# Experts: the down product transposed, in three f32r passes, its input split by ScalarE and GpSimd

## What is computed

```python
y = einsum('nei,ne,ehi->nh', silu(hg) * hu, cw, Wd)      # 16 experts of 64 hidden features
shared = silu(xf @ Ws_g.T) * (xf @ Ws_u.T) @ Ws_d.T      # one of 128
return x + (x + y + shared)                              # and then the layer norm
```

## Time and profile before

| | |
|---|---|
| median of 3 runs | 646.74 us (644.06 to 647.41) |
| the profiled execution | 647.47 us, its span 645.7 us |
| mean granted TensorE clock | 0.961 |
| TensorE busy | 578.3 us (90%), weight loads 481.1 us |
| VectorE, ScalarE, GpSimd busy | 474.1 us (73%), 277.2 us (43%), 208.1 us (32%) |
| experts stage | first pass at 442.06 us, last residual addition at 637.3 us |

### The profile page before, as it was taken

The page is one execution under the profiler, slowest core; times in us unless marked ns, Lnnn a source line. Parts: engine busy times, 40 slices in busy tenths (PEclk is TensorE's granted clock), DMA queues, the critical chain, the costliest instruction groups (busy, mean ns, idle before and its releaser), DMA issues. The chain is left out here.

```text
span 645.7 us, 17900 instructions
## 1 busy us (share of the span) xinstructions
PE 578.3 (90%) x6280; PEld 481.1 (74%) x6280; DVE 474.1 (73%) x1174; ACT 277.2 (43%) x544; POOL 208.1 (32%) x260
## 2 busy tenths in 40 slices
PE   5769999999999745999999998887999999999994
PEld 5647777787787543777788786676888888888884
DVE  2858977977988645677887887564887887888863
ACT  2365645655654401654655563453233233233220
POOL 4233304414421577324345436732021020120122
PEclk9979999999999975899999999898999999999998
DMA  7222122111211554245446537000010100000000
GB/s 221 63 78 78 37 63 65 59 45 58 65 50 34 153 144 100 70 139 171 123 151 169 140 97 218 11 5 32 2 33 2 33 32 0 32 32 0 18 17 16
DMA packets 43086, 46.13 MB, mean 71 GB/s; under 512 B 5056, under 2 KB 31328, under 8 KB 43024
## 3 DMA queue, kind: packets, MB, share of 16 engines
q1 hardware_dynamic: 41104, 42.57, 22.5%
q0 software_dynamic: 704, 1.92, 1.1%
q10 hardware_dynamic: 1216, 0.79, 0.5%
HBM read 32.48 MB, written 10.94 MB: 67 GB/s over the span
## 5 line engine op out<-in xcount | busy, mean ns | idle before, releaser
L1953 PE MATMUL bank<-xT_hl_c,w_up 128*128 128x512 f32 x432 | 119.6, 413 | 2.4 <-ACTq L67 2.4
L141 POOL TENSOR_TENSOR rstd<-mv,norm_c 128x4 f32<-128x4 f32 x24 | 5.2, 216 | 290.9 <-DVE mv L135 183.7
L1278 DVE TENSOR_REDUCE nmax<-bank 128x4 f32<-128x512 f32 x112 | 72.0, 684 | 27.9 <-PE bank L1434 24.6
L1186 ACT ACTIVATE prob<-bank 128x512 f32<-128x512 f32 x128 | 69.4, 594 | 51.3 <-PE bank L1434 35.6
L1953 PEld LDWEIGHTS bank<-xT_hl_c,w_up 128*128 128x128 f32 x432 | 77.3, 192 | 16.3 <-ACTq L67 2.7
L1875 ACT ACTIVATE sg<-bank 128x512 f32<-128x512 f32 x72 | 43.0, 597 | 106.6 <-PE bank L1953 104.7
L1969 PEld LDWEIGHTS bank<-w_down,hid 128*128 128x128 f32 x576 | 74.4, 191 | 6.0 <-issue 0.5
L1969 PE MATMUL bank<-w_down,hid 128*128 128x128 f32 x576 | 75.6, 275 | 0.0
L1424 PE MATMUL bank<-neg_i,mask 64*128 64x256 bf16 x512 | 52.1, 283 | 15.2 <-ACT prob L1186 6.0
L1908 DVE TENSOR_TENSOR gu<-sg,bank 128x512 f32<-128x512 f32 x64 | 43.8, 685 | 21.7 <-PE bank L1953 10.5
L1912 DVE TENSOR_TENSOR hid<-gu,bank 128x512 f32<-128x512 f32 x64 | 44.0, 687 | 6.5
(11 more groups left out here) (219 smaller groups left out, 1174.1 us busy)
## 6 DMA issues: line engine op xcount, KB each, us to landing
rows<-sum_rows_scratch SPq DMA_DIRECT2D x32, 256.0 KB, 3.2
k_stack<-k_scratch SPq DMA_DIRECT2D x32, 128.0 KB, 2.9
q_stack<-q_scratch SPq DMA_DIRECT2D x32, 128.0 KB, 2.8
k_scratch<-k_part SPq DMA_DIRECT2D x16, 192.0 KB, 2.4
q_scratch<-q_part SPq DMA_DIRECT2D x16, 192.0 KB, 2.5
x<-xT_in SPq DMA_DIRECT2D x8, 256.0 KB, 8.4
mask<-mask_in SPq DMA_DIRECT2D x8, 256.0 KB, 3.0
xres<-x_in SPq DMA_DIRECT2D x8, 256.0 KB, 3.7
```

Source lines behind the costliest of these rows:

```text
L1186: act.activation(prob[:, b % 2, ORDER[n], :, :], (TT0, TT1)[n % 2][:, :], ACT.Exp, scale=XD ** -0.5)\
L1278: dve.tensor_reduce(nmax[:, b, 4 * u:4 * u + 4], (SS0, SS1)[n % 2][:, :].rearrange("p (i k) -> p i k", i=4), AX_X, ALU.max, negate=True).t ...
L1953: mm = pe.matmul(bank[:, :], w_up[:, which, a, c, :], xT_hl[par][:, v, :], start=(n == 0), stop=(n == 2))
```

## The change

The down product is turned round: `w_down` is the weights and the hidden activations move, in three f32r passes of 512 columns a chunk, into `PO` with the features in the partitions. For this `hid` is split: ScalarE copies it into a high f32r part (`hidden_hi`), GpSimd subtracts it to get the low part (`hidden_lo`), both into `hid_hl`, a ring of three chunks. `hid` is now a ring of three as well. Down runs three chunks behind up. Since `PO` is now transposed, ScalarE copies it to `outT` and TensorE turns it back in four transposes into `PF` (`output`), a bank that the preparation of the next groups uses too; the residual addition reads `PF`. `w_down` is split once at the start. The preparation moves: the x2 transposes for group `g + 2` now come in the last chunks of group `g`, and four chunks of the next group come before the residual.

```diff
@@ -1800,6 +1800,7 @@
+    LAG, RING = 3, 3
     with ExitStack() as ctx:
@@ -1812,10 +1813,13 @@
         xT_hl.append(sb("xT_hl_c1", [P, 2, GT], F32R))
+        w_down_hl = sb("w_down_hl", [P, 2, NC, P], F32R)
         xs = sb("xs_c", [P, 2, GS, P])
...
         gu = sb("gu", [P, 2, GT])
-        hid = sb("hid", [P, NC, GT])
+        hid = sb("hid", [P, RING, GT])
+        hid_hl = sb("hid_hl", [P, RING, 2, GT], F32R)
+        outT = sb("outT", [P, GT])
         res, stats, mv, rstd = t["res"], t["stats"], t["mv"], t["rstd"]
@@ -1823,7 +1827,10 @@
         p_g, p_d, a_s = sem("gate_mm", NC), sem("down_mm", NC), sem("silu_ready", NC)
+        p_t, a_o = sem("out_transposed"), sem("outT_copied")
         v_gu, v_hid = sem("gu_ready", NC), sem("hid_ready", CHUNKS)
+        a_h, g_l = sem("hid_hi", NC), sem("hid_lo", NC)
+        w_parts = raw("w_down_parts")
         v_res, g_out, x2_out = sem("res_c_ready", 1 + 2 * GS), sem("out_ready", 4), t["x2_out"]
@@ -1856,17 +1863,33 @@
             g_out.prime(pool)
+            g_l.prime(pool)
...
+            def hidden_lo(g, c):
+                pool.wait_ge(a_h.sem, a_h.at(g, c))
+                pool.tensor_tensor(hid_hl[:, c % RING, 1, :], hid[:, c % RING, :], hid_hl[:, c % RING, 0, :].bitcast(F32),
+                                   ALU.subtract).then_inc(g_l.sem, 1)
...
             def group(g, par, left):
+                for c in range(LAG + 1, NC):
+                    hidden_lo(g, c)
+                if left:
+                    for c in range(LAG + 1):
+                        hidden_lo(g + 1, c)
                 normalise_pool(pool, g, v_res, g_out, res, mv, rstd, norm_c, normed[:, par, :, :],
...
+            pool.wait_ge(w_parts, 1)
+            pool.tensor_tensor(w_down_hl[:, 1], w_down[:, :, :], w_down_hl[:, 0].bitcast(F32), ALU.subtract).then_inc(w_parts, 1)
             normalise_pool(pool, NG - 1, t["x2_res"], x2_out, res, mv, rstd, norm_c, x2[:, NSEQ - GS:, :])
+            for c in range(LAG + 1):
+                hidden_lo(0, c)
             pairs(pool, group)
...
         def _(act):
-            a_s.prime(act)
+            for s in (a_s, a_h, a_o):
+                s.prime(act)
@@ -1874,21 +1897,49 @@
+            def hidden_hi(g, c):
+                done = (v_hid, c - 1) if c else (v_gu, 0)
+                act.wait_ge(done[0].sem, done[0].at(g, done[1]))
+                act.wait_ge(p_d.sem, p_d.at(g, c - RING))
+                act.activation(hid_hl[:, c % RING, 0, :], hid[:, c % RING, :], ACT.Copy).then_inc(a_h.sem, 1)
...
+            def output_copy(g):
+                act.wait_ge(p_d.sem, p_d.at(g, NC - 1))
+                act.wait_ge(p_t.sem, p_t.at(g - 1))
+                act.activation(outT[:, :], PO[:, :], ACT.Copy).then_inc(a_o.sem, 1)
...
             def group(g, par, left):
                 nxt = (g + 1, 1 - par)
-                for c in range(2, NC):
+                for c in range(LAG + 1, NC):
                     silu(g, par, c)
-                    if left and c == 2:
-                        x2T_hi(act, e, *nxt)
-                    if left and c == 3:
+                    hidden_hi(g, c - 1)
+                    if left and c == LAG + 1:
                         logit_tanh(act, e, g + 1)
...
                     copy_weights(act, e, *nxt)
+                hidden_hi(g, NC - 1)
+                if left:
                     silu(*nxt, 1)
...
+                    hidden_hi(g + 1, 0)
+                    silu(*nxt, 2)
+                output_copy(g)
+                if left == 2:
+                    x2T_hi(act, e, g + 2, par)
+                if left:
+                    hidden_hi(g + 1, 1)
+                    silu(*nxt, 3)
+                    hidden_hi(g + 1, 2)
...
+            act.activation(w_down_hl[:, 0], w_down[:, :, :], ACT.Copy).then_inc(w_parts, 1)
             silu(0, 0, 0)
             silu(0, 0, 1)
+            hidden_hi(0, 0)
+            silu(0, 0, 2)
+            x2T_hi(act, e, 1, 1)
+            hidden_hi(0, 1)
+            silu(0, 0, 3)
+            hidden_hi(0, 2)
             pairs(act, group)
@@ -1901,7 +1952,7 @@
                 dve.wait_ge(p_u.sem, p_u.at(g, c))
-                dve.wait_ge(p_d.sem, p_d.at(g - 1, c))
+                dve.wait_ge(g_l.sem, g_l.at(g, c - RING))
                 if c:
@@ -1909,35 +1960,40 @@
                     dve.wait_ge(p_w.sem, p_w.at(g, c - 1))
-                    dve.tensor_tensor(hid[:, c, :], gu[:, k, :], WW[(c - 1) % 2][:, :], ALU.mult).then_inc(v_hid.sem, 1)
+                    dve.tensor_tensor(hid[:, c % RING, :], gu[:, k, :], WW[(c - 1) % 2][:, :], ALU.mult).then_inc(v_hid.sem, 1)
...
                 nxt = (g + 1, 1 - par)
-                for c in range(2, NC):
+                for c in range(LAG + 1, NC):
                     hidden(g, par, c)
-                    if left and c == 2:
-                        x2T_lo(dve, e, *nxt)
-                    if left and c == 3:
+                    if left and c == LAG + 1:
                         expert_scores(dve, e, g + 1)
                         rank_groups(dve, e, g + 1)
-                    if left and c == 5:
+                    if left and c == LAG + 3:
                         select_experts(dve, e, g + 1)
-                    if left and c == 7:
+                    if left and c == LAG + 4:
                         share_weights(dve, e, g + 1)
...
                     hidden(*nxt, 1)
-                dve.wait_ge(p_d.sem, p_d.at(g, NC - 1))
-                residual_dve(dve, g, PO, x2[:, bass.ds(g * GS, GS), :], g_out, v_res, dve_passed, res, stats, mv, times=2.0)
+                    hidden(*nxt, 2)
+                    if left == 2:
+                        x2T_lo(dve, e, g + 2, par)
+                    hidden(*nxt, 3)
+                dve.wait_ge(p_t.sem, p_t.at(g))
+                residual_dve(dve, g, PF, x2[:, bass.ds(g * GS, GS), :], g_out, v_res, dve_passed, res, stats, mv, times=2.0)
...
             hidden(0, 0, 1)
+            hidden(0, 0, 2)
+            x2T_lo(dve, e, 1, 1)
+            hidden(0, 0, 3)
             dve.wait_ge(x2_out.sem, x2_out.at(NG - 1, 3))
...
         def _(pe):
-            for s in (p_g, p_d):
+            for s in (p_g, p_d, p_t):
                 s.prime(pe)
@@ -1959,36 +2015,56 @@
             def down(g, c):
+                pe.wait_ge(g_l.sem, g_l.at(g, c))
                 if c == 0:
-                    pe.wait_ge(v_gu.sem, v_gu.at(g, 0))
-                    pe.wait_ge(v_res.sem, v_res.at(g - 1, 0))
-                else:
-                    pe.wait_ge(v_hid.sem, v_hid.at(g, c - 1))
+                    pe.wait_ge(a_o.sem, a_o.at(g - 1))
+                for n, (a, v) in enumerate(((0, 0), (1, 0), (0, 1))):
+                    mm = pe.matmul(PO[:, :], w_down_hl[:, a, c, :], hid_hl[:, c % RING, v, :],
+                                   start=(c == 0 and n == 0), stop=(c == NC - 1 and n == 2))
+                mm.then_inc(p_d.sem, 1)
...
+            def output(g, freed):
+                pe.wait_ge(a_o.sem, a_o.at(g))
+                pe.wait_ge(*freed)
                 for b in range(GS):
...
-                    mm = pe.matmul(PO[:, b * P:(b + 1) * P], hid[:, c, b * P:(b + 1) * P], w_down[:, c, :],
-                                   start=(c == 0 and b == 0), stop=(c == NC - 1), skip_group_check=True)
-                mm.then_inc(p_d.sem, 1)
+                    mm = pe.transpose(PF[:, b * P:(b + 1) * P], outT[:, b * P:(b + 1) * P], ident32[:, :])
+                mm.then_inc(p_t.sem, 1)
...
                 nxt = (g + 1, 1 - par)
-                for c in range(2, NC):
+                for c in range(LAG + 1, NC):
                     up(g, par, c)
-                    down(g, c - 2)
-                    if left and c == 2:
-                        x2T(*nxt)
-                    if left and c == 3:
+                    down(g, c - LAG)
+                    if left and c == LAG + 1:
+                        pe.wait_ge(v_res.sem, v_res.at(g - 1, 0))
                         expert_logits(pe, e, g + 1)
...
                     transpose_weights(pe, e, g + 1)
+                down(g, NC - 3)
+                if left:
+                    up(*nxt, 1)
                 down(g, NC - 2)
                 if left:
-                    up(*nxt, 1)
+                    up(*nxt, 2)
+                if left == 2:
+                    x2T(g + 2, par)
                 down(g, NC - 1)
+                if left:
+                    up(*nxt, 3)
+                if not left:
+                    pe.wait_ge(v_res.sem, v_res.at(g - 1, 0))
+                output(g, (e.a_f.sem, e.a_f.at(g + 2)) if left == 2 else (a_c.sem, a_c.at(g + 1)) if left else (a_c.sem, a_c.at(g)))
+                if left:
+                    down(g + 1, 0)
...
             up(0, 0, 1)
+            up(0, 0, 2)
+            x2T(1, 1)
+            up(0, 0, 3)
+            pe.wait_ge(w_parts, 2)
+            down(0, 0)
             pairs(pe, group)
```

## The result

| | before | after |
|---|---|---|
| median of 4 runs each | 647.08 us (644.06 to 647.92) | 689.34 us (687.41 to 694.72) |
| ratio | | 1.0664, 95% interval 1.0623 to 1.0706 |
| profiled execution, its span | 647.47, 645.7 us | 688.5, 686.8 us |
| granted TensorE clock | 0.961 | 0.938 |
| first residual of the experts after the last one of the attention stage | 472.08 - 439.2 = 32.9 us | 484.34 - 441.7 = 42.6 us |

A forecast was written before the change was run, and what follows sets the result against it. TensorE was taken to bound the experts stage, with VectorE close behind. First group +7.3, groups 1 to 5 +27, group 6 +3.5, last -3.4 sum to +34.4 on 647.47: 682 us, range 653 to 698.

The forecast's parts named there:

- The bound: Experts stage: TensorE bounds it at 24.33 us a group; the change takes it to 21.5, below VectorE's 22.7.
- The slack of VectorE: Experts stage: VectorE's stretches sum to 22.7 of 24.33 us, so it allows a gain of 1.6 a group at most.
- T to s, 16.6: From VectorE's start of chunk 4 (T) to the end of the shares (s): 13.3 us plus 3.3 of collisions.
- s to T', 13.1: From the shares' end through transposes, down 8, ScalarE's copies and chunk 3 to the residual: 13.1 us.
- Collisions, 3.3: VectorE's small two-tensor operations in ranks, selection and shares wait for whole GpSimd operations: +3.3 us a group.
- the upper bound of 4.4: Collisions cost up to 4.4 us a group if MAX8 and MATCH_REPLACE wait for GpSimd as well.
- Rival 1: Few collisions: GpSimd mostly misses VectorE's small operations, leaving the chain of waits alone; 660 us, chance 0.21.
- Rival 3: TensorE's clock falls after pauses of about 3 us; +2.0 in each of seven groups, +14, 696 us; chance 0.13.
- The forecast case: Whole kernel: the chain of waits plus collisions makes the period 29.7 us, +5.4, and the time 682 us; chance 0.50.
- The sum: Whole kernel: 7.3 + 27 + 3.5 - 3.4 = +34.4 us on the profiled 647.47, giving 682 us.
- the first group's +7.3: First group: +5.4, less 0.9 without normalisation before it, plus 2.8 for the residual two chunks later in VectorE's order.
- Rivals 2 and 4: 2: VectorE runs without pause at 22.7 us, 634, chance 0.10. 4: period 24.3, time near 647, chance 0.06.

The follow-up runs named there:

- e7: The changed kernel with every down pass run twice, three passes more a chunk: 705.69 us, ratio 1.0918 to the kernel before.
- e5: The kernel before plus eight GpSimd subtractions of 128x512 a group on spare tensors, which no engine waits for: 662.74 us, ratio 1.0232.
- e4: The changed kernel, all work kept, with GpSimd made to wait until VectorE's chains are past: 662.84 us, ratio 1.0236 to the kernel before.
- e3: The changed kernel reordered: x2 transposes behind up 1, their ScalarE copies ahead of silu 2 and outT, x2T_lo between chunks 1 and 2: 686.74 us.
- e9: Changed kernel with GpSimd waits, earlier x2T, down 6 before the shares' transposes, chunk 4's subtraction before L148, silu 1 before chunk 8's high copy: 651.29 us.

## Why the prediction was right, and where it was off

*The bound.* Right: TensorE falls below VectorE, and e7 shows it has room. The slack of VectorE in the kernel before was put too high: its stretches (they add to 22.6, not 22.7) leave 1.6 us of 24.33 only if it never waits. e5 made VectorE's chain 2.7 us longer and the period grew by 2.45, so some 0.3 was to be had.

*T to s, 16.6; s to T', 13.1.* Measured in the group shown: 16.5 and 13.4. The wait of x2T_lo was put at 1.7 and is 1.57, six times. The difference of 0.3 in the second part has a wait in it that the prediction did not name: GpSimd does two subtractions in a row there, and chunk 2's `gu` waits 0.69 for its ring buffer.

*Collisions, 3.3.* Right in place and size: L148 and the subtractions of chunks 4, 5 and 7 meet the four operations that they were said to meet (3.15 in the group shown; e4 takes 3.15 to 3.3 off five of six groups). MAX8 and MATCH_REPLACE do not wait for GpSimd: four MAX8 take 0.41 beside a subtraction, and their mean is 164 ns in both kernels. This settles the upper bound of 4.4. Rival 1 (few collisions, 660) is refuted.
The Trainium skill's page "SBUF — State Buffer", SBUF: two separate sides, which the prediction used for operations with two SBUF inputs, also names VectorE operations in a two-port mode. In e5 `score`, with one SBUF input, takes 0.80 us beside a subtraction and 0.20 alone; no trace names the mode, so that it runs in such a one is not shown. In the changed kernel `score` met none.

*The clock.* Rival 3 had the mechanism (a fall behind a pause of 3 us) and the place: a fall behind the second pause does lie on the loop. It had the price and the number wrong: +2.0 in seven groups were foreseen, measured are 1.4 in group 2 and 1.3 in the first group. In the others the fall comes behind the first pause and fills the second, the argument against the rival, as the group shown does. The forecast case put the clock at nothing; it was 2.7 us. It is not a constant: in e3 the fall lies behind the shares in three of the six groups at 1.4 to 1.5 each.

*The sum.* 682 us were forecast and 689.34 measured, inside the range. The profiled execution, 688.5, is 6.6 above by steps: the six groups 31.6 in place of 30.5 (27 and 3.5), of which 1.4 is the clock in group 2, the first group 9.7 in place of 7.3, the last -2.8 in place of -3.4, and 2.5 ahead of the experts, where nothing was changed and the profiles of all kernels vary by as much. The mis-sized term is the first group's +7.3. Its collisions were as foreseen (one operation of the ranks at 1.20, `open_` 0.80, `cw` 1.02, 2.3 in all). 1.3 of the missing 2.4 goes with the half clock behind the first group's pause before the shares (granted 0.50 from 472 to 475 us): chunk 1's `gu` waits 2.07 for its silu, where e4, whose first group has no such fall, waits 0.77. For the other 1.1 no cause is shown; it is neither the clock nor a collision, since the first group of e4, which has neither, is 6.0 longer than before where the sum without collisions gives 2.1 + 2.8 = 4.9.

*Rivals 2 and 4* (634 and 647) are refuted for this kernel. How fast the change would be without any collision stays open: e9 is 4 us above the kernel before, and 1.1 of the 1.9 us by which its period exceeds the 22.7 of serial work is the holding of x2T_lo and `score`.

## What to carry to other kernels

Before moving work from TensorE to GpSimd, look at what VectorE does in those microseconds: a GpSimd operation of 1.3 us on two SBUF tensors turns each small VectorE operation on two SBUF tensors that it meets into one of up to 1.3 us, and in a chain that is pure delay. Choosing when GpSimd starts was worth 26 us here for four waits. And after an engine has lost its place as the bound, a saving on the chain must be tried with TensorE's clock kept up before it is called worthless: e3 alone showed 0.07 us a group, with the pauses filled 0.72. Read the groups one by one: here a mean of six hid that the clock costs 1.4 us in one of them and nothing in the others.
